# Attention on one Trainium2 core: weights times values in 512-query pieces, sums turned one head later, one norm spread over the steps

## The chip, the cores and the metric

One NeuronCore of one Trainium2 chip. The metric is the device time of one execution in microseconds. The kernel runs a chain of four layers on a sequence of 2 x 1024 tokens of width 256; the change touches only the last layer.

## The reference, cut to what it computes

```
x: 2 batches x 1024 tokens x 256
x = layer0(x); x = layer1(x); x = layer2(x)      # linear attention, two state-space layers
# layer 3, 16 heads of width 16
xn = layer_norm(x) * w + b
q, k, v = xn @ q_w + q_b, xn @ k_w + k_b, (xn @ v_w + v_b) * mask
att = softmax(q k^T + (1 - mask) * -1e6)          # per head, 1024 x 1024
y = att v                                         # per head, 1024 x 16
h = layer_norm(y) * g(cond) + h(cond)             # the norm called lny3 below
x + silu(h) @ out_w + out_b
```

## The kernel before, in words

Layer 3 handles 32 heads (2 batches x 16). Four heads make a unit (u = 0 to 7; units 0 to 3 are batch 0), and a unit has eight steps (mt = 0 to 7), one for each tile of 128 keys. So there are 64 steps, and in each the four heads j = 0 to 3 are taken in turn. All engines follow one written order; semaphores (`w.wait_ge`) join them.

For one head in one step TensorE computes the scores of 128 keys against 1024 queries: two bf16 matmuls of 512 columns (L1546) into a pair of PSUM banks. There are two such pairs (the ring `doubles`), so a pair is taken only when ScalarE has done the exponential of the head two places before (L1582, one ACTIVATE of 128x1024). The exponentials (the "weights") of one step lie in SBUF and are multiplied with the values in the step after it: `weigh_t` (L1408) does this as fp32 matmuls, the four heads side by side in four 32-column tiles of the array. Each fp32 matmul appears as two records. Before, `weigh_t(.., c)` handles 256 queries and one quarter c is issued at each head j, between the second trial and the second score matmul.

The exponential needs the maximum of each row, and that is computed ahead, LEAD = 40 items before it is used. An item is 128 queries of one head: two "trial" matmuls of 512 keys (L1360), each into one bank of a ring of only two (`first`), and two VectorE reductions (L1373, 128x512 from PSUM), each of which gives its bank back. One item goes with each head of each step, for the first 54 steps. Every eighth item also turns the collected maxima: an fp32 transpose (L1322) that takes a bank of the same ring, a copy on VectorE (L1328), and small work on GpSimd (L1336 to L1342) and two DMAs that bring the row into the operand of the scores.

The order on TensorE for one head is therefore: trial 0, score 0, trial 1, quarter c = j of the weights times values of the step before, score 1.

At the end of a unit the sums lie in two PSUM banks (PV). ScalarE copies one (`normalise_s`, L1425), VectorE the other (L1432), TensorE turns them with eight fp32 transposes into a pair of the ring `doubles` (`normalise_t`, L1418), and VectorE divides by the sum (L1437, L1440) and so frees the pair. Before, all of this stands after head 3 of the first step of the next unit.

When batch 0 is complete, its tail is put between the steps of units 5 and 6 (`tail_due`): lny3 of batch 0 after step (5, 1), its transposes and Silu after (5, 4), the four output products after (5, 7) to (6, 7). lny3 is `norm_v`: eight bn_stats (L205), eight bn_aggr (L208), one add (L210), a power on GpSimd (`norm_p`, L218), and eight tensor_scalar (L213) that subtract and scale; before, all but the power is VectorE's, in one piece. Batch 1 has its tail at the end.

Of the kernel before, what the change touches and what calls it, by code (L numbers as in the profile page):

```python
# [8 lines left out]
ALU = mybir.AluOpType  # L9
# [5 lines left out]
TB = S // 128  # L15
# [92 lines left out]
def program(nc, T, out):  # L108
    with ExitStack() as ctx:
# [18 lines left out]
        ST = sb("ST", [128, NT, 6])  # L128
        MV = sb("MV", [128, NT, 2])
# [67 lines left out]

        def norm_v(e, w, tag, src, dst, tiles, wait):  # L200
            a, b = tiles[0], tiles[-1] + 1
            w.wait_ge(*dve.now())
            for i in tiles:
                wait(i)
                e.bn_stats(ST[:, i, :], src(i)).then_inc(*dve.up((tag, "stats", i)))  # L205
            for i in tiles:
                w.wait_ge(*dve.at((tag, "stats", i)))
                e.bn_aggr(MV[:, i, :], ST[:, i, :]).then_inc(*dve.up())  # L208
            w.wait_ge(*dve.now())
            e.tensor_scalar(VE[:, a:b], MV[:, a:b, 1], EPS, None, ALU.add).then_inc(*dve.up((tag, "var")))  # L210
            w.wait_ge(*pool.at((tag, "rsqrt")))
            for i in tiles:
                e.tensor_scalar(dst(i), src(i), MV[:, i, 0:1], RS[:, i:i + 1], ALU.subtract, ALU.mult).then_inc(*dve.up((tag, i)))  # L213

        def norm_p(e, w, tag, tiles):
            a, b = tiles[0], tiles[-1] + 1
# [8 lines left out]
        def turn_t(e, w, tag, src, chunks, wait, ring=banks):  # L225
            for c in chunks:
                for h in range(2):
                    o = take(w, (tag, c, h), ring)
                    for j in range(4):
                        wait(4 * c + j)  # L230
                        t = e.transpose(o[:, j * 128:(j + 1) * 128], src(4 * c + j, h), ident[:, :])
                    t.then_inc(*pe.up((tag, c, h)))
# [1166 lines left out]
        def weigh_t(e, w, u, mt, c):  # L1399
            b, g = units[u]  # L1400
            for j in range(HQ):
                h, tile = HQ * g + j, b * TB + mt
                if mt == 0 and u:
                    w.wait_ge(*act.at(("lower", u - 1)))
                    w.wait_ge(*dve.at(("upper", u - 1)))
                w.wait_ge(*act.at(("weights", u, mt, j)))
                w.wait_ge(*act.at(("v3", tile)))
                t = e.matmul(PV[32 * j:32 * j + 32, c // 2, c % 2 * 256:c % 2 * 256 + 256], V[:, tile * 272 + 17 * h:tile * 272 + 17 * h + 32],  # L1408
                             PX[mt % 2][j][:, c * 256:(c + 1) * 256], start=mt == 0 and c % 2 == 0, stop=mt == TB - 1, tile_position=(0, 32 * j),
                             skip_group_check=True)  # L1410
            t.then_inc(*pe.up(("weighed", u, mt, c)))

# [6 lines left out]
            t.then_inc(*pe.up(("turned", u)))  # L1419

        def normalise_s(e, w, u):
            w.wait_ge(*pe.at(("weighed", u, TB - 1, 3)))
            if u:
                w.wait_ge(*pe.at(("turned", u - 1)))
            e.activation(PVs[:, 0:512], PV[:, 0, :], ACT.Copy).then_inc(*act.up(("lower", u)))  # L1425

        def normalise_v(e, w, u):
            b, g = units[u]
            w.wait_ge(*pe.at(("weighed", u, TB - 1, 3)))
            if u:  # L1430
                w.wait_ge(*pe.at(("turned", u - 1)))
            e.tensor_copy(PVs[:, 512:1024], PV[:, 1, :]).then_inc(*dve.up(("upper", u)))  # L1432
            i = banks.place.get(("turned", u), 2)
            f4 = PS[:, i:i + 2, :].rearrange("p a (q j e) -> p (a q) j e", j=HQ, e=32)
            w.wait_ge(*pe.at(("turned", u)))
            w.wait_ge(*dve.now())
            e.reciprocal(RC, f4[:, :, :, 16]).then_inc(*dve.up())  # L1437
            w.wait_ge(*dve.now())
            y = Yt[:, b * TB:(b + 1) * TB, HQ * 16 * g:HQ * 16 * (g + 1)].rearrange("p q (j e) -> p q j e", j=HQ)
            e.tensor_tensor(y, f4[:, :, :, 0:16], RC.unsqueeze(3).broadcast_to([128, TB, HQ, 16]), ALU.mult).then_inc(*dve.up(("y3", u)))  # L1440
            banks.give(("turned", u), dve.now())
# [2 lines left out]

        def tail_t(e, w, b, n, ring):
            if n == 1:
                turn_t(e, w, ("sn3", b), lambda i, h: Yt[:, i, h * 128:(h + 1) * 128], (2 * b, 2 * b + 1), lambda i: w.wait_ge(*dve.at((("lny3", b), i))), ring)
            if n >= 2:
                i = b * TB + 2 * (n - 2)
                w.wait_ge(*act.at((("sn3", b), i // 4, 1)))  # L1450
                tokens_t(e, w, ("o3", i), lambda k, i: SN[b][k][i // 4 % 2][:, i % 4 * 128:(i % 4 + 1) * 128], 2, lambda k: Wo[:, k, :], "l3bo",
                         (i, i + 1), ring)
# [44 lines left out]
        def layer3_p(e, w):  # L1497
            layer2_done(w)
            e.memset(V, 1.0).then_inc(*pool.up("v_ones"))
            norm3_p(e, w, 1)  # L1500
            for job in front_jobs(0):
                if not isinstance(job, int) and job[3] and job[4] and on_pool(*job[0:3]):
                    rest_of_parts(e, w, job, pool)
            todo = front_jobs(1)
            for i in range(LEAD):
                ahead_p(e, w, i)
                if i < len(todo) and not isinstance(todo[i], int) and todo[i][3] and todo[i][4]:
                    rest_of_parts(e, w, todo[i], pool)
            for u, mt, last in steps():
                for j in range(HQ):  # L1510
                    ahead_p(e, w, LEAD + 32 * u + 4 * mt + j)
                if tail_due(u, mt) is not None:
                    tail_p(e, w, 0, tail_due(u, mt))
            for n in range(6):
                tail_p(e, w, 1, n)

        def layer3_t(e, w):
# [17 lines left out]
            for u, mt, last in steps():  # L1535
                for j in range(HQ):
                    k = HQ * u + j
                    sl = k % SLOTS
                    key = ("score", u, mt, j)
                    take(w, key, doubles)  # L1540
                    for c in range(2):
                        ahead_t(e, w, LEAD + 32 * u + 4 * mt + j, (c,))
                        if c == 1 and last:
                            weigh_t(e, w, *last, j)
                        w.wait_ge(*transfer(f"max_row{sl}").at(k))
                        t = e.matmul(PS[:, banks.place[key] + c, :], SK3[sl][0:102, mt * 128:(mt + 1) * 128], SQ[sl][0:102, c * 512:(c + 1) * 512],  # L1546
                                     start=True, stop=True)
                    t.then_inc(*pe.up(key))
                    if last and j == 3 and last[1] == TB - 1:
                        normalise_t(e, w, last[0])  # L1550
                if tail_due(u, mt) is not None:
                    tail_t(e, w, 0, tail_due(u, mt), doubles)
            for c in range(4):
                weigh_t(e, w, len(units) - 1, TB - 1, c)
            normalise_t(e, w, len(units) - 1)
            w.wait_ge(*dve.at(("y3", len(units) - 1)))
# [4 lines left out]
        def layer3_s(e, w):  # L1561
# [12 lines left out]
            for u, mt, last in steps():  # L1574
                for j in range(HQ):
                    key = ("score", u, mt, j)
                    i = banks.place.get(key, 2)
                    w.wait_ge(*pe.at(key))
                    step = 8 * u + mt
                    if step >= 2:  # L1580
                        w.wait_ge(*pe.at(("weighed", (step - 2) // 8, (step - 2) % 8, 3)))
                    e.activation(PX[mt % 2][j], PS[:, i:i + 2, :].rearrange("p a b -> p (a b)"), ACT.Exp).then_inc(*act.up(("weights", u, mt, j)))  # L1582
                    banks.give(key, act.now())
                    if last and j == 3 and last[1] == TB - 1:
                        normalise_s(e, w, last[0])
                if tail_due(u, mt) is not None:
                    tail_s(e, w, 0, tail_due(u, mt))
            normalise_s(e, w, len(units) - 1)
# [3 lines left out]
        def layer3_v(e, w):  # L1592
# [14 lines left out]
            for u, mt, last in steps():  # L1607
                for j in range(HQ):
                    for c in range(2):
                        ahead_v(e, w, LEAD + 32 * u + 4 * mt + j, (c,))  # L1610
                    if last and j == 3 and last[1] == TB - 1:
                        normalise_v(e, w, last[0])
                if tail_due(u, mt) is not None:
                    tail_v(e, w, 0, tail_due(u, mt))
            normalise_v(e, w, len(units) - 1)
            for n in range(6):
                tail_v(e, w, 1, n)
# [132 lines left out]
```

## Time and profile before

| | |
|---|---|
| time, median of 3 runs | 2215.05 us (2214.99 to 2222.23) |
| profiled execution, its own time | 2217.42 us |
| its span, first to last instruction | 2215.7 us |
| mean granted TensorE clock | 0.949 |
| attention steps, first to last exponential | 1715.1 to 2183.1 us |
| one step, from first exponential to first exponential | 6.69 or 6.91 us (with a turn of maxima) |
| DVE, ACT, POOL busy over 1713 to 2186 us (473 us) | 309.25, 271.11, 40.81 us |

A row of the timeline gives the start, the length, the engine, the line, the operation and its operands, and how often it was merged; in brackets stands how long the engine was idle before it and what released it. PE is TensorE's matmul, PEld its weight load, DVE VectorE, ACT ScalarE, POOL GpSimd; x8 means eight records merged into one row. The records of matmuls are longer than the spacing of their starts, because matmuls are pipelined; so the starts are what is to be compared. PEclk is the granted clock of TensorE: 1.00 is 2.4 GHz, 0.50 is 1.2 GHz.

### The profile page before, as it was taken

How to read it: one execution, taken by the hardware profiler on the slowest of the kernel's cores; microseconds unless marked ns; L12 is line 12 of the kernel's file. 1: busy time of each engine (PE TensorE's matmuls, PEld its weight loads, DVE VectorE, ACT ScalarE, POOL GpSimd, SP SyncE). 2: the span in 40 equal slices, each digit the busy share in tenths (PEclk: the TensorE clock that was granted, in tenths of full speed). 3: DMA queues.
4: the chain of work that ended last, by engine and by line, in shares of the span. 5: the costliest groups of instructions: out<-in, count | busy, mean ns of one | idle time of the engine just before them, and what ended most of it. 6: DMA issues, size and time to landing. Idle time of an engine off the chain costs nothing.

```text
span 2215.7 us, 34737 instructions
## 1 busy us (share of the span) xinstructions
PE 2018.9 (91%) x13528; PEld 1417.9 (64%) x13528; DVE 1613.1 (73%) x2067; ACT 1438.8 (65%) x2422; POOL 1061.2 (48%) x594
## 2 busy tenths in 40 slices
PE   6969799887998899989999999899988999998997
PEld 4844699737997499759984899599842222332333
DVE  5554699447996499769984899599768777776621
ACT  3314799347983699589845997799642655554564
POOL 1021499405994199639950799299624100111000
PEclk9989799987999899999999999999998999998998
DMA  4040111101111011102100111111101111111000
GB/s 175 1 141 20 43 58 58 41 13 55 58 57 50 20 54 58 35 23 55 54 24 2 49 58 49 35 54 58 29 22 38 30 29 30 29 28 30 9 20 20
DMA packets 54161, 95.04 MB, mean 43 GB/s; under 512 B 11815, under 2 KB 20167, under 8 KB 52590
## 3 DMA queue, kind: packets, MB, share of 16 engines
q1 hardware_dynamic: 52462, 88.63, 13.2%
q0 software_dynamic: 1536, 4.20, 0.6%
q8 instruction: 107, 1.75, 0.3%
q14 instruction: 56, 0.46, 0.1%
HBM read 73.29 MB, written 6.91 MB: 36 GB/s over the span
## 4 chain that ended last, share of the span: by engine, by line
PE 66%; POOL 8%; ACT 8%; DVE 8%; issue 8%; DMA 1%; SPq 0%; POOLq 0%; DVEq 0%; ACTq 0%
PE PS L723 11%; PE PS L745 11%; POOL A L857 7%; PE PS L1408 6%; PE PS L253 5%; PE PS L1360 5%; PE PS L1546 5%; PE PS L728 5%; PE PS L244 4%; PE PS L608 2%; PE PS L751 2%; ACT A L809 2%; PE PS L1090 1%; DVE A L1029 1%; DVE A L1373 1%
## 5 line engine op out<-in xcount | busy, mean ns | idle before, releaser
L857 POOL TENSOR_TENSOR A<-A 128x1024 f32<-128x1024 f32 x384 | 897.9, 2391 | 138.1 <-ACT small L798 126.1
L809 ACT ACTIVATE A<-A,negA 128x512 f32<-128x512 f32 x768 | 546.6, 712 | 42.5 <-DVE A L842 32.9
L842 DVE TENSOR_TENSOR_SCAN A<-A,PS 128x512 f32<-128x512 f32 x384 | 434.4, 1199 | 55.0 <-ACT A L809 36.3
L842 DVE TENSOR_TENSOR_SCAN A<-A,small,PS 128x512 f32<-128x512 f32 x384 | 455.2, 1256 | 6.1 <-PE PS L723 5.5
L745 PE MATMUL PS<-ident,A 128*128 128x128 f32 x3072 | 401.3, 273 | 18.8 <-POOL A L857 13.8
L1582 ACT ACTIVATE A<-PS 128x1024 f32<-128x1024 f32 x256 | 262.2, 1024 | 222.0 <-PE PS L1546 220.4
L723 PE MATMUL PS<-A 128*128 128x128 f32 x3072 | 392.4, 280 | 5.6 <-DVE A L842 5.6
L1373 DVE TENSOR_REDUCE A<-PS 128x1 f32<-128x512 f32 x512 | 329.8, 686 | 80.7 <-PE PS L1360 77.3
L723 PEld LDWEIGHTS PS<-A 128*128 128x128 f32 x3072 | 371.5, 196 | 14.2 <-DVE A L842 7.8
L745 PEld LDWEIGHTS PS<-ident,A 128*128 128x128 f32 x3072 | 346.6, 141 | 28.8 <-POOL A L857 19.0
L783 ACT ACTIVATE A<-A,small 128x512 f32<-128x512 f32 x340 | 239.9, 710 | 24.3 <-PE PS L728 20.2
L728 PE MATMUL PS<-ident,A 128*128 128x128 f32 x1360 | 195.5, 282 | 24.7 <-ACT A L783 23.8
L1360 PE MATMUL PS<-A 99*128 99x512 bf16 x480 | 189.4, 401 | 8.0 <-DVE A L1373 7.2
L1408 PE MATMUL PS<-A,W 128*32 128x256 f32 x2048 | 192.5, 397 | 1.7 <-ACT A L1582 1.7
L1546 PE MATMUL PS<-A 102*128 102x512 bf16 x480 | 184.9, 392 | 0.1
L728 PEld LDWEIGHTS PS<-ident,A 128*128 128x128 f32 x1360 | 163.0, 146 | 32.9 <-issue 22.8
L790 ACT ACTIVATE A<-ident,small 128x128 f32<-128x128 f32 x384 | 147.4, 388 | 7.5 <-PE PS L723 6.7
L218 POOL TENSOR_TENSOR RS<-VE,HALF 128x8 f32<-128x8 f32 x14 | 23.0, 1644 | 265.6 <-DVE VE L210 265.6
L685 POOL TENSOR_TENSOR A<-A 128x2048 f32<-128x2048 f32 x6 | 32.2, 5374 | 241.8 <-ACT A L647 241.8
L244 PE MATMUL PS<-A,W 128*128 128x512 f32 (+1 forms) x288 | 132.0, 616 | 8.9 <-ACT A L1014 6.6
L1546 PEld LDWEIGHTS PS<-A 102*128 102x128 bf16 x480 | 46.4, 98 | 126.2 <-issue 100.6
L1408 PEld LDWEIGHTS PS<-A,W 128*32 128x32 f32 x2048 | 47.8, 109 | 121.6 <-issue 99.3
(198 smaller groups left out, 2045.5 us busy)
## 6 DMA issues: line engine op xcount, KB each, us to landing
A<-scrc SPq DMA_DIRECT2D x192, 256.0 KB, 3.1
A<-A SPq DMA_DIRECT2D x360, 32.0 KB
scr<-A SPq DMA_DIRECT2D x4, 1024.0 KB, 4.6
W<-in_wa SPq DMA_DIRECT2D x2, 1536.0 KB, 10.1
X<-in_x SPq DMA_DIRECT2D x4, 512.0 KB, 5.4
out<-X SPq DMA_DIRECT2D x2, 1024.0 KB, 4.5
W<-in_w SPq DMA_DIRECT2D x1, 1984.0 KB, 8.3
W<-in_wzc SPq DMA_DIRECT2D x1, 1536.0 KB, 11.8
```

What stands on the lines that cost most here:

```text
L723: t = e.matmul(o[:, j * 128:(j + 1) * 128], r.DUT[:, 4 * ci + j, dt * 128:(dt + 1) * 128], DB[k // 2 % 2][:, j, :], start=True, stop=True)
L728: t = e.transpose(o[:, j * 128:(j + 1) * 128], r.G[(2 * k + j) % 6][:, dt * 128:(dt + 1) * 128], ident[:, :])
L745: t = e.matmul(PS[:, j, dt * 128:(dt + 1) * 128], r.H[pair % HS][:, dt % 2, j * 128:(j + 1) * 128], ident[:, :], start=open_y(ci, j), stop ...
L783: e.activation(r.G[(2 * k + j) % 6], r.DUT[:, 4 * ci + j, :], ACT.Copy, scale=Bt[:, 4 * ci + j, s:s + 1]).then_inc(*scaled.up((q, k, j)))
L809: e.activation(A_B[i % 4], r.DT[:, dt, ci * 512:(ci + 1) * 512], ACT.Exp, scale=negA[:, r.n, dt * 16 + s:dt * 16 + s + 1]).then_inc(*decay ...
L842: e.tensor_tensor_scan(h, a, u, init, ALU.mult, ALU.add).then_inc(*scanned.up((q, i)))
L857: e.tensor_tensor(h, h, CB[k % 2].unsqueeze(1).broadcast_to([128, 2, 512]), ALU.mult).then_inc(*weighed.up((q, pair)))
L1360: e.matmul(o, SQ[j][0:99, nt * 128:(nt + 1) * 128], SK3[j][0:99, c * 512:(c + 1) * 512], start=True, stop=True).then_inc(*pe.up(("trial", ...
L1373: e.tensor_reduce(NM[:, k % 2, q:q + 1], bank(("trial", k, nt, c)), AX.X, ALU.max, negate=True).then_inc(*dve.up(("trial", k, nt, c)))
L1408: t = e.matmul(PV[32 * j:32 * j + 32, c // 2, c % 2 * 256:c % 2 * 256 + 256], V[:, tile * 272 + 17 * h:tile * 272 + 17 * h + 32], PX[mt % ...
L1546: t = e.matmul(PS[:, banks.place[key] + c, :], SK3[sl][0:102, mt * 128:(mt + 1) * 128], SQ[sl][0:102, c * 512:(c + 1) * 512], start=True, ...
L1582: e.activation(PX[mt % 2][j], PS[:, i:i + 2, :].rearrange("p a b -> p (a b)"), ACT.Exp).then_inc(*act.up(("weights", u, mt, j)))
```

## The change

1. `weigh_t` handles 512 queries instead of 256: `c` runs over 2 instead of 4, one PSUM bank each. It is issued at j = 1 (c = 0) and j = 3 (c = 1) only.
2. The end of a unit is spread. The copy by ScalarE comes before the exponential of head 3 of step (u, 0), the copy by VectorE after the reductions of that head, and the transposes and the division one head later, at j = 0 of step (u, 1).
3. lny3 of batch 0: two bn_stats after each of the steps (4, 3) to (4, 6), the aggregation after (4, 7), the power and the eight tensor_scalar on GpSimd, there too. Batch 1's norm keeps its order.

```diff
+        def stats_v(e, tag, src, tiles):
+            for i in tiles:
+                e.bn_stats(ST[:, i, :], src(i)).then_inc(*dve.up((tag, "stats", i)))
...
+        def moments_v(e, w, tag, tiles):       # the bn_aggr and the add of norm_v, moved here
...
-                t = e.matmul(PV[32 * j:32 * j + 32, c // 2, c % 2 * 256:c % 2 * 256 + 256], V[:, tile * 272 + 17 * h:tile * 272 + 17 * h + 32],
-                             PX[mt % 2][j][:, c * 256:(c + 1) * 256], start=mt == 0 and c % 2 == 0, stop=mt == TB - 1, tile_position=(0, 32 * j),
+                t = e.matmul(PV[32 * j:32 * j + 32, c, :], V[:, tile * 272 + 17 * h:tile * 272 + 17 * h + 32],
+                             PX[mt % 2][j][:, c * 512:(c + 1) * 512], start=mt == 0, stop=mt == TB - 1, tile_position=(0, 32 * j),
...
         def normalise_v(e, w, u):              # the copy is now take_upper_v
-            w.wait_ge(*dve.now())
+            if u:
+                w.wait_ge(*dve.at(("y3", u - 1)))
...
 # layer3_p
-                if tail_due(u, mt) is not None:
-                    tail_p(e, w, 0, tail_due(u, mt))
+                if u == 4 and mt == 7:
+                    tail_p(e, w, 0, 0)
+                    w.wait_ge(*pool.at((("lny3", 0), "rsqrt")))
+                    for i in range(TB):
+                        e.tensor_scalar(Yt[:, i, :], Yt[:, i, :], MV[:, i, 0:1], RS[:, i:i + 1], ALU.subtract, ALU.mult).then_inc(*pool.up(("lny3", 0, i)))
...
 # layer3_t
-                        if c == 1 and last:
-                            weigh_t(e, w, *last, j)
+                        if c == 1 and last and j % 2:
+                            weigh_t(e, w, *last, j // 2)
...
-                    if last and j == 3 and last[1] == TB - 1:
-                        normalise_t(e, w, last[0])
+                    if j == 0 and u and mt == 1:
+                        normalise_t(e, w, u - 1)
...
 # layer3_s
+                    if j == 3 and u and mt == 0:
+                        normalise_s(e, w, u - 1)
                     w.wait_ge(*pe.at(key))
...
-                    if last and j == 3 and last[1] == TB - 1:
-                        normalise_s(e, w, last[0])
...
 # layer3_v
-                    if last and j == 3 and last[1] == TB - 1:
-                        normalise_v(e, w, last[0])
-                if tail_due(u, mt) is not None:
+                    if j == 3 and u and mt == 0:
+                        take_upper_v(e, w, u - 1)
+                    if j == 0 and u and mt == 1:
+                        normalise_v(e, w, u - 1)
+                if u == 4 and 3 <= mt < 7:
+                    w.wait_ge(*dve.at(("y3", 3)))
+                    stats_v(e, ("lny3", 0), lambda i: Yt[:, i, :], (2 * mt - 6, 2 * mt - 5))
+                if u == 4 and mt == 7:
+                    moments_v(e, w, ("lny3", 0), range(TB))
+                if tail_due(u, mt):
                     tail_v(e, w, 0, tail_due(u, mt))
```

## Rows read from the trace of the kernel before

**Rows 1.** Two heads of a regular step, TensorE, VectorE and ScalarE (timeline).

```profile
1803.45 0.38 PE L1360 MATMUL PS<-A 99*128 99x512 bf16 x1
1803.76 0.64 PE L1408 MATMUL PS<-A,W 128*32 128x256 f32 x8
1804.33 0.39 PE L1546 MATMUL PS<-A 102*128 102x512 bf16 x1
1804.56 0.38 PE L1360 MATMUL PS<-A 99*128 99x512 bf16 x1
1804.76 1.02 ACT L1582 ACTIVATE A<-PS 128x1024 f32<-128x1024 f32 x1 [0.52 <-PE PS L1546]
1804.97 1.29 DVE L1373 TENSOR_REDUCE A<-PS 128x1 f32<-128x512 f32 x2 [0.26 <-PE PS L1360]
...
1805.83 0.14 PEld L1408 LDWEIGHTS PS<-A,W 128*32 128x32 f32 x2 [0.38 <-ACT A L1582]
```

**Rows 2.** First exponential of two steps that lie two apart, ScalarE (timeline).

```profile
1799.90 1.02 ACT L1582 ACTIVATE A<-PS 128x1024 f32<-128x1024 f32 x1 [1.03 <-PE PS L1546]
...
1813.50 1.02 ACT L1582 ACTIVATE A<-PS 128x1024 f32<-128x1024 f32 x1 [1.03 <-PE PS L1546]
```

**Rows 3.** A whole fp32 matmul of 512 columns and its successor, TensorE (timeline).

```profile
1660.00 1.02 PE L1248 MATMUL PS<-A,W 128*128 128x512 f32 x2
1660.87 0.73 PE L1360 MATMUL PS<-A 99*128 99x512 bf16 x2
```

**Rows 4.** A bank given back by VectorE and the weight load behind it (timeline).

```profile
1786.41 0.28 DVE L1328 COPY W<-PS 8x128 f32<-8x128 f32 x1 [0.66 <-PE PS L1322]
...
1786.74 0.10 PEld L1360 LDWEIGHTS PS<-W 99*128 99x128 bf16 x1 [0.43 <-DVE W L1328]
```

**Rows 5.** End of unit 0, all three engines (timeline).

```profile
1769.88 1.02 ACT L1582 ACTIVATE A<-PS 128x1024 f32<-128x1024 f32 x1 [1.03 <-PE PS L1546]
...
1774.32 0.39 PE L1546 MATMUL PS<-A 102*128 102x512 bf16 x1
...
1775.66 0.59 ACT L1425 ACTIVATE W<-PS 128x512 f32<-128x512 f32 x1
...
1776.40 1.06 PE L1418 MATMUL PS<-ident,W 128*128 128x128 f32 x8 [1.69 <-ACT W L1425]
...
1779.04 1.02 ACT L1582 ACTIVATE A<-PS 128x1024 f32<-128x1024 f32 x1 [2.79 <-PE PS L1546]
...
1786.30 1.02 ACT L1582 ACTIVATE A<-PS 128x1024 f32<-128x1024 f32 x1 [1.03 <-PE PS L1546]
```

**Rows 6.** First exponential after the end of unit 3, ScalarE (timeline).

```profile
1952.29 1.02 ACT L1582 ACTIVATE A<-PS 128x1024 f32<-128x1024 f32 x1 [4.36 <-PE PS L1546]
```

**Rows 7.** Around lny3 of batch 0 (timeline).

```profile
2015.40 2.71 DVE L205 BATCH_NORM_STATS2 ST<-A 128x6 f32<-128x256 f32 x8
...
2017.26 1.02 ACT L1582 ACTIVATE A<-PS 128x1024 f32<-128x1024 f32 x1 [1.03 <-PE PS L1546]
...
2020.61 2.67 DVE L213 TENSOR_SCALAR A<-A,MV,RS 128x256 f32<-128x256 f32 x8 [1.75 <-POOL RS L218]
...
2030.41 1.02 ACT L1582 ACTIVATE A<-PS 128x1024 f32<-128x1024 f32 x1 [1.81 <-PE PS L1546]
...
2034.10 1.02 ACT L1582 ACTIVATE A<-PS 128x1024 f32<-128x1024 f32 x1 [1.03 <-PE PS L1546]
```

**Rows 8.** Two stretches (windows): us; PE, PEld, DVE, ACT, POOL busy; PEclk; DMA; GB/s.

```profile
1706.00:1712.00 6.00, 5.26 (x9) 0.83 (x9) 5.59 (x9) 0.00 (x0) 0.00 (x0) 0.50 0.17 39
...
2024.00:2030.00 6.00, 5.77 (x25) 1.26 (x26) 3.43 (x6) 1.02 (x1) 1.40 (x4) 0.50 0.12 28
```

**Rows 9.** First exponentials of two steps without trials, ScalarE (timeline).

```profile
2151.81 2.13 ACT L1582 ACTIVATE A<-PS 128x1024 f32<-128x1024 f32 x2 [1.03 <-PE PS L1546]
...
2157.36 2.13 ACT L1582 ACTIVATE A<-PS 128x1024 f32<-128x1024 f32 x2 [1.03 <-PE PS L1546]
```

**Rows 10.** GpSimd's elementwise work in the layers before (page, costliest groups).

```profile
L857 POOL TENSOR_TENSOR A<-A 128x1024 f32<-128x1024 f32 x384 | 897.9, 2391 | 138.1 <-ACT small L798 126.1
```

More of the change, by code:

```diff
@@ L204, in norm_v @@
                 wait(i)
-                e.bn_stats(ST[:, i, :], src(i)).then_inc(*dve.up((tag, "stats", i)))
+                stats_v(e, tag, src, (i,))
+            moments_v(e, w, tag, tiles)
+            w.wait_ge(*pool.at((tag, "rsqrt")))
+            for i in tiles:
+                e.tensor_scalar(dst(i), src(i), MV[:, i, 0:1], RS[:, i:i + 1], ALU.subtract, ALU.mult).then_inc(*dve.up((tag, i)))
+        def moments_v(e, w, tag, tiles):
+            a, b = tiles[0], tiles[-1] + 1
             for i in tiles:
@@ L210, in norm_v @@
             e.tensor_scalar(VE[:, a:b], MV[:, a:b, 1], EPS, None, ALU.add).then_inc(*dve.up((tag, "var")))
-            w.wait_ge(*pool.at((tag, "rsqrt")))
-            for i in tiles:
-                e.tensor_scalar(dst(i), src(i), MV[:, i, 0:1], RS[:, i:i + 1], ALU.subtract, ALU.mult).then_inc(*dve.up((tag, i)))
         def norm_p(e, w, tag, tiles):
@@ L1421, in normalise_s @@
         def normalise_s(e, w, u):
-            w.wait_ge(*pe.at(("weighed", u, TB - 1, 3)))
+            w.wait_ge(*pe.at(("weighed", u, TB - 1, 1)))
             if u:
@@ L1425, in normalise_s, with take_upper_v @@
             e.activation(PVs[:, 0:512], PV[:, 0, :], ACT.Copy).then_inc(*act.up(("lower", u)))
-        def normalise_v(e, w, u):
-            b, g = units[u]
-            w.wait_ge(*pe.at(("weighed", u, TB - 1, 3)))
+        def take_upper_v(e, w, u):
+            w.wait_ge(*pe.at(("weighed", u, TB - 1, 1)))
             if u:
@@ L1432, in normalise_v @@
             e.tensor_copy(PVs[:, 512:1024], PV[:, 1, :]).then_inc(*dve.up(("upper", u)))
+        def normalise_v(e, w, u):
+            b, g = units[u]
             i = banks.place.get(("turned", u), 2)
@@ L1446, in tail_t @@
             if n == 1:
-                turn_t(e, w, ("sn3", b), lambda i, h: Yt[:, i, h * 128:(h + 1) * 128], (2 * b, 2 * b + 1), lambda i: w.wait_ge(*dve.at((("lny3", b), i))), ring)
+                turn_t(e, w, ("sn3", b), lambda i, h: Yt[:, i, h * 128:(h + 1) * 128], (2 * b, 2 * b + 1), lambda i: w.wait_ge(*(dve if b else pool).at((("lny3", b), i) if b else ("lny3", 0, i))), ring)
             if n >= 2:
@@ L1548, in layer3_t @@
                     t.then_inc(*pe.up(key))
-                    if last and j == 3 and last[1] == TB - 1:
-                        normalise_t(e, w, last[0])
+                    if j == 0 and u and mt == 1:
+                        normalise_t(e, w, u - 1)
                 if tail_due(u, mt) is not None:
                     tail_t(e, w, 0, tail_due(u, mt), doubles)
-            for c in range(4):
+            for c in range(2):
                 weigh_t(e, w, len(units) - 1, TB - 1, c)
@@ L1580, in layer3_s @@
                     if step >= 2:
-                        w.wait_ge(*pe.at(("weighed", (step - 2) // 8, (step - 2) % 8, 3)))
+                        w.wait_ge(*pe.at(("weighed", (step - 2) // 8, (step - 2) % 8, 1)))
                     e.activation(PX[mt % 2][j], PS[:, i:i + 2, :].rearrange("p a b -> p (a b)"), ACT.Exp).then_inc(*act.up(("weights", u, mt, j)))
                     banks.give(key, act.now())
-                    if last and j == 3 and last[1] == TB - 1:
-                        normalise_s(e, w, last[0])
                 if tail_due(u, mt) is not None:
@@ L1610, in layer3_v @@
                         ahead_v(e, w, LEAD + 32 * u + 4 * mt + j, (c,))
-                    if last and j == 3 and last[1] == TB - 1:
-                        normalise_v(e, w, last[0])
-                if tail_due(u, mt) is not None:
+                    if j == 3 and u and mt == 0:
[8 more added lines that the diff above has]
+                if tail_due(u, mt):
                     tail_v(e, w, 0, tail_due(u, mt))
+            take_upper_v(e, w, len(units) - 1)
             normalise_v(e, w, len(units) - 1)
```

## The prediction

> **What bounds the kernel now.** I read the page for where the time lies, then the timeline of the attention steps engine by engine, then windows for the granted clock. The reader is to look at starts, not lengths. In a regular step TensorE is the bound: from the trial at 1803.45 to the scores at 1804.33 and the next trial at 1804.56 nothing but issue stands between matmuls, and a head repeats after 1.54 us (the exponential takes 1.02 after 0.52 us of idling for its scores) [rows 1]. Of that, four bf16 matmuls take 0.22 each and the quarter of the weights times values 0.66 (1803.45 to 1804.33, less 0.22). Once in a step it also waits: the first quarter needs the exponential of head 3, started just before: its last weight load comes at 1805.83, when that exponential (1804.76 + 1.02) ends [rows 1], and the next exponential then idles 1.03 instead of 0.52 [rows 2]. That makes 3 x 1.545 + 2.05 = 6.69 us a step; two steps take 13.60 [rows 2], so one with a turn of maxima takes 6.91. VectorE's two reductions take 1.29 of the 1.54 us [rows 1]: close behind.
>
> **The weights times values alone.** A quarter is four fp32 matmuls side by side. A whole fp32 matmul of 512 columns passes in 0.87 us [rows 3], so 256 columns stream in 0.43, and 0.66 - 0.43 = 0.23 us is fixed: 0.09 on entry (0.31 from the trial to it, less 0.22), the rest inside and on leaving. A half of 512 columns should cost 0.86 + 0.23 = 1.09, of which 1.00 from its own start to the scores behind it. Two halves are 2.18 us a step against 2.64: 0.46 less. Also the half now stands at head 1, when the exponential of head 3 is long done: 0.51 less. On TensorE's account a step falls from 6.69 to 5.72. No row shows four side by side at 512 columns. From below it can't be under its streaming, 0.86; from above, a half costs two quarters from start to scores, 2 x 0.57 = 1.14 [rows 1]. I take 1.00, since streaming scaled in rows 3.
>
> **What the step really does then.** The trials have two banks. Count from trial 0 of an even head, which has no half: its reductions start 0.42 later and take 1.29 [rows 1], and a bank given back lets the next weight load start 0.05 later [rows 4]. So trial 1 of the odd head, which needs the second of these banks, starts at 0.42 + 1.29 + 0.05 = 1.76, although TensorE would be there at 1.3. Then the half: 0.31 to its start, 1.00 to score 1, 0.22 to the next trial. A pair of heads takes 3.30 and a step 6.59, against 6.69. In a step with a turn of maxima the turn takes one of the two banks, so the gate moves from trial 1 to trial 0, 0.44 earlier in the order: 6.59 + 0.44 = 7.03, against 6.91. The steps alternate, so the two cancel (-0.10 and +0.12, some 20 pairs: **+0.5**). Nearly the whole 0.97 us per step is given to this gate: before, a quarter lay at every head and covered it; now even heads have no cover and odd heads have twice too much. The first step loses a wait and gains **-0.8**.
>
> **End of a unit.** Before: two steps take 16.42 us (1769.88 to 1786.30) where 13.60 is regular [rows 2, 5], 2.8 more. TensorE idles from 1774.54 (0.22 after the scores) to 1776.40, for the exponential of head 3 and ScalarE's copy behind it, then works 0.90 on the transposes, and the trial behind waits for the division on VectorE. After: ScalarE copies (0.59 [rows 5]) between the end of the half and the exponential of head 3, which so starts 0.45 after score 1 (0.43 before [rows 1]) and ends at 1.47. TensorE goes on with head 0 of the next step and is through at 0.22 + 4 x 0.22 = 1.10; the transposes then take the pair of banks that this exponential gives back, so they wait some 0.4 and take 0.9. The gate of the next odd head, 0.3 or so, would have been waited for anyway. That is 1.0 more than regular, so -1.8 for each of six ends, and -0.7 at the last, where no trials lie: **-11.5**; I take **-11**.
>
> **The norm.** Before, lny3 holds VectorE for 7.9 us in one piece, 2015.40 to 2023.28, with the two reductions waiting behind it and TensorE behind them; the step takes 16.84 (2017.26 to 2034.10) [rows 7]. Afterwards it is a regular 7.03: **-9.8**, of which 2.6 is half clock after the stall: PEclk is 0.50 from 2024 to 2030 [rows 8], and a head takes 1.81 + 1.02 = 2.83 us there [rows 7] instead of 1.54, twice. What comes instead: two bn_stats in each of four steps, 0.68 us (2.71 for eight [rows 7]) behind the last reduction, on the gate's chain only in part: **+0.4**. The subtraction on GpSimd: from below as VectorE, 2.7 us for eight [rows 7]; from above as its two-input work, 2.39 us per 1024 elements [rows 10], 4.8 for eight, with its start some 6. Its results are first needed after step (5, 4), 30 us later, and the row maxima queued behind it on GpSimd are for a head used 40 items later. Cost nothing; if a step did wait, at most these 6 us.
>
> **Tail of batch 0 and the steps without trials.** Six pieces lie between steps; after each the first head has no half, so the gate is not covered: 0.4 each, **+2.3**. After Silu the exponential's table returns while TensorE now has no quarter to do: **+0.8**. From the last trial on, a pair of heads must wait for the exponential two places before: 1.02 + 0.05 + 1.31 + 0.43 = 2.81, a step 5.62 against 5.56 [rows 1, 9]; and the last step's halves both lie behind its last exponential's partner: **+1.8** together.
>
> **Clock at the ends of units.** At the end of unit 3 the exponentials idle for 4.36 us [rows 6] where they idle for 2.79 at the end of unit 0 [rows 5]. The work is the same; the 1.6 us are half clock, and the end of unit 4 has them too. With 0.4 us idle instead of 1.9 I expect both gone: **-3.2** (bound: 0).
>
> **Sum.** +0.5 - 0.8 - 11 - 9.8 + 0.4 + 2.3 + 0.8 + 1.8 - 3.2 = **-19.0 us**. The profiled execution (2217.4, span 2215.7) would be 2198.4; it lies 2.4 above the median, which becomes 2196. 0.5% (11 us) is what a measurement of this kernel can tell from no change.
>
> **A rule that speaks against it.** With the gate, TensorE waits on PSUM banks twice in each pair of heads. While trials ran alone, gated in just that way, PEclk was 0.50 [rows 8]. The Trainium skill (TensorE: Matmul & The Clock Gate, "A second HAM failure mode: psum-queue depth-cycling") says that such short idles between groups can make the clock fall and rise again. By that rule the steps would pay the half clock often, as in rival 3. I give it little, because the new step streams 16 x 0.22 + 2 x 0.86 = 5.2 of its 6.6 us [rows 1, 3]; the old one streamed the same in 6.7, without losing the clock.
>
> **Rivals.**
> 1. The half is dear, or a release takes longer than 0.05. With 1.14 for 1.00 each of some 125 halves costs 0.14 on the chain: +18, so 2214. Halfway: 2205. For it: nobody ran this form. Against: rows 3. Chance 0.20, ends within 0.5%.
> 2. The whole gain on TensorE arrives, since the gate is less tight than I count: 0.97 x 54 steps = 52 instead of nothing, 2145. Against it stand VectorE's 1.29 us and two banks. Chance 0.04.
> 3. **The other side:** the clock falls to 1.2 GHz in the steps because of the gate's idles. At half clock a head takes 2.83 us instead of 1.54 [rows 1, 7], 1.3 more. From 15 of the 256 heads on the gain of 19 is gone, from 23 on the kernel is slower by over 0.5%; with one head in six halved it is 43 x 1.3 = +56 on 2196, 2252. Chance 0.06.
> 4. The norm's new places hurt: GpSimd's 6 us are waited for, and the statistics fall wholly on the chain (4 x 0.7): +9, 2205. Chance 0.08, within or just faster.
>
> **How the numbers follow.** The forecast, 2196, has 0.62. Its own terms leave -12 to -26. Range 2184 to 2213: below, the half at its streaming (-0.1 x 125 = -12); above, rival 1 nearly whole. Faster by over 0.5%: the forecast, rival 2, and some of 1 and 4: 0.72; same: 0.21; slower: 0.07.
>
> **What would show it.** Half to scores 1.00 us; regular steps 6.6 and 7.0, with idle time before the odd heads' trial 1 put down to the reduction; ends of units 14.6 for two steps; step (5, 1) near 7.0; no PEclk under 1 at the ends of units 3 and 4. The forecast is wrong if steps are near 5.8 (the gate isn't one) or over 6.8 (half or release dearer), or if PEclk falls in regular steps.

## The result, and the profile after

The changed kernel takes 2203.06 us (median of 6 runs, 2194.13 to 2205.47), the kernel before on the same chip 2216.49 (6 runs, 2213.74 to 2223.2): a ratio of 0.9924, 95% interval 0.9899 to 0.9949. It is faster by 0.76%. The prediction said 2196 with a range of 2184 to 2213: right in direction and range, 7 us too low. In a later series of runs, against the kernel before of that series, it stands at 0.9900 (0.9867 to 0.9933).

Two questions follow. Did the gain come from where the prediction put it? And why did the time fall by 13.4 us and not by 19?

**Where the time went.** The two kernels share all code up to the attention stage. I take the stretch from the first exponential to the last from ScalarE's timeline; it holds all that the change touches but the end of the last unit. Before it runs from 1715.06 to 2183.11, 468.0 us. After:

```profile
1723.11 1.02 ACT L1598 ACTIVATE A<-PS 128x1024 f32<-128x1024 f32 x1 [24.16 <-PE PS L1560]
...
2171.86 1.02 ACT L1598 ACTIVATE A<-PS 128x1024 f32<-128x1024 f32 x1 [0.89 <-PE PS L1560]
```

That is 448.8 us, 19.3 less by the unrounded records; the forecast sum was 19.0. But the first exponential comes 8.05 us later than before, in code that nobody changed. Windows of both kernels over layer 2 show the clearest part of it (us; PE, PEld, DVE, ACT, POOL busy; PEclk; DMA; GB/s), after and then before:

```profile
1390.00:1412.00 22.00, 21.48 (x37) 8.33 (x38) 7.09 (x9) 14.34 (x16) 0.00 (x0) 0.61 0.02 4
```

```profile
1389.00:1411.00 22.00, 21.36 (x55) 8.31 (x55) 11.90 (x10) 18.25 (x21) 4.32 (x1) 1.00 0.02 4
```

The reader is to see the same place in the program at PEclk 0.61 against 1.00. The chain that ended last has the same 16 matmuls there (one line of the program, eight lines lower in the changed file), after and before:

```profile
1390.52 11.55 PE PS L616 x16
...
1422.62 1.93 PE PS L1098 x4
```

```profile
1389.64 7.13 PE PS L608 x16
...
1413.52 1.93 PE PS L1090 x4
```

From the first row to the last the changed kernel falls from 0.88 us behind to 9.10 us behind. So the profiled execution after (2205.47, span 2203.7) is 12.0 us under the one before (2217.42, span 2215.7), and not 19: 19.3 less the 8.05, and 0.7 us that it is shorter behind the last exponential (31.9 for 32.6).

**The regular step.** TensorE, VectorE and ScalarE in two heads of the changed kernel (timeline), which answer to [rows 1] and [rows 2]:

```profile
1821.77 0.38 PE L1368 MATMUL PS<-A 99*128 99x512 bf16 x1
1821.99 0.38 PE L1560 MATMUL PS<-A 102*128 102x512 bf16 x1
1822.21 0.38 PE L1368 MATMUL PS<-A 99*128 99x512 bf16 x1
1822.43 0.38 PE L1560 MATMUL PS<-A 102*128 102x512 bf16 x1
1823.05 0.39 PE L1368 MATMUL PS<-A 99*128 99x512 bf16 x1 [0.24 <-ACT A L1598]
1823.28 0.38 PE L1560 MATMUL PS<-A 102*128 102x512 bf16 x1
1823.53 0.39 PE L1368 MATMUL PS<-A 99*128 99x512 bf16 x1
1823.85 1.06 PE L1416 MATMUL PS<-A,W 128*32 128x512 f32 x8
1824.85 0.39 PE L1560 MATMUL PS<-A 102*128 102x512 bf16 x1
```

```profile
1821.97 1.94 ACT L1598 ACTIVATE A<-PS 128x1024 f32<-128x1024 f32 x2 [1.81 <-PE PS L1560]
1822.19 2.58 DVE L1381 TENSOR_REDUCE A<-PS 128x1 f32<-128x512 f32 x4 [0.68 <-PE PS L1368]
1823.53 0.10 PEld L1368 LDWEIGHTS PS<-A 99*128 99x128 bf16 x1 [0.37 <-DVE A L1381]
1825.28 1.94 ACT L1598 ACTIVATE A<-PS 128x1024 f32<-128x1024 f32 x2 [1.37 <-PE PS L1560]
```

The half goes from its start to the scores in 1.00 us (1823.85 to 1824.85), as forecast from a whole matmul [rows 3]. Then two rings are to be read. A ring is here a set of banks that are used in turn, and its length is the time from the taking of a bank to the moment at which the same bank can be taken again. Both come to 3.3 us for a pair of heads.

- The trials' banks: trial 0 of the even head at 1821.77, its reductions from 1822.19 (0.42), two of them 1.29, the next weight load at 1823.53 (0.05): 1.76 us, to the hundredth what was forecast. Then 0.32, 1.00 and 0.22 to the next even head: 3.30.
- The scores' banks: the exponential of the odd head starts at 1821.97 and takes 1.02; 0.06 later, at 1823.05, the next odd head's trial 0 starts, for in program order the head takes its pair of score banks ahead of its trials. Then 0.23 + 0.25 + 0.32 + 1.00 to the last scores and 0.43 to their exponential at 1825.28: 3.31, of which 0.03 is the wait of trial 1 for the first ring.

The prediction saw the first and not the second, and in these heads the idle time stands at the second's place. The waits over 1723 to 2172 (us in total, times, longest) say so for the whole stage, in which the waits for the reduction are the fewer:

```profile
PE PS L1368 <- ACT A L1598: 15.8, 65, 0.2
PE PS L1368 <- DVE A L1381: 6.3, 27, 0.6
```

**The steps.** Durations from first exponential to first exponential. A regular step takes 6.62 and one with a turn of maxima 7.05, against 6.69 and 6.91. Sorted by the prediction's terms, with the differences of all 64 steps (steps beside a piece of the tail count as tail, those at the end of a unit as ends):

| term | forecast | measured |
|---|---|---|
| regular steps | +0.5 | +0.9 (34 steps) |
| first step | -0.8 | -1.0 |
| ends of units with their half clock | -11 - 3.2 | -13.2 (-1.6 for each of units 0 to 2, -2.6, -2.7, -1.1, -1.9) |
| norm's step | -9.8 | -9.8 (16.85 to 7.06) |
| statistics | +0.4 | +0.2 |
| tail pieces, table | +2.3 + 0.8 | +1.8 |
| steps without trials, last step | +1.8 | +1.8 (0.09 for each of six, 1.2) |
| sum | -19.0 | -19.3 |

An end of a unit on TensorE and ScalarE (timeline), which answers to [rows 5]:

```profile
1838.52 0.39 PE L1560 MATMUL PS<-A 102*128 102x512 bf16 x1
1838.66 0.60 ACT L1433 ACTIVATE W<-PS 128x512 f32<-128x512 f32 x1 [1.08 <-PE PS L1416]
1839.15 1.94 ACT L1598 ACTIVATE A<-PS 128x1024 f32<-128x1024 f32 x2
1840.22 1.09 PE L1426 MATMUL PS<-ident,W 128*128 128x128 f32 x8 [0.44 <-ACT A L1598]
1841.15 0.38 PE L1368 MATMUL PS<-A 99*128 99x512 bf16 x1
```

TensorE idles 0.44 us in front of the transposes, where it idled 1.69 in [rows 5] (the row's own mark), and the trial follows at once. The exponential after the end of unit 3 idles 2.24 us where it idled 4.36 [rows 6], the same as after unit 1:

```profile
1843.33 2.03 ACT L1598 ACTIVATE A<-PS 128x1024 f32<-128x1024 f32 x2 [2.24 <-PE PS L1560]
...
1954.94 2.03 ACT L1598 ACTIVATE A<-PS 128x1024 f32<-128x1024 f32 x2 [2.24 <-PE PS L1560]
```

The half clock is gone from the ends. The stage begins at half clock in both kernels (until 1727.6 here and 1719.8 before, by the clock's records). After that it falls in one place only. The windows show the whole stage and the stretch with that place (columns as above):

```profile
1723.00:2172.00 449.00, 400.28 (x2091) 110.04 (x2093) 303.43 (x528) 257.62 (x269) 50.23 (x121) 0.99 0.11 25
...
2034.00:2048.00 14.00, 11.52 (x61) 4.56 (x53) 6.13 (x11) 10.06 (x11) 0.00 (x0) 0.88 0.00 0
```

The second holds the tail's transposes and Silu, not regular steps.

### The profile page after: what moved, and what is told of

Same layout as the page of the kernel before. It is cut to its first block, busy times and chain, and to the rows that moved or that the text cites. A ratio compares the mean times of both kernels' runs of the same rounds, so it can differ in the third digit from the quotient of the medians.

```text
span 2203.7 us, 32728 instructions
## 1 busy us (share of the span) xinstructions
PE 1984.2 (90%) x12504; PEld 1392.5 (63%) x12504; DVE 1609.2 (73%) x2059; ACT 1426.4 (65%) x2422; POOL 1068.6 (48%) x602
## 3 DMA queue, kind: packets, MB, share of 16 engines
q1 hardware_dynamic: 52462, 88.63, 13.4%
HBM read 73.29 MB, written 6.91 MB: 36 GB/s over the span
## 4 chain that ended last, share of the span: by engine, by line
PE 63%; ACT 11%; DVE 9%; POOL 8%; issue 7%; DMA 1%; SPq 0%; POOLq 0%; DVEq 0%; ACTq 0%
PE PS L731 11%; PE PS L753 11%; POOL A L865 7%; PE PS L261 5%; PE PS L736 5%; PE PS L1416 5%; PE PS L1368 4%; PE PS L252 4%; ACT A L1598 4%; PE PS L1560 3%; DVE A L1381 3%; PE PS L616 2%; PE PS L759 2%; ACT A L817 2%; PE PS L1098 2%
## 5 line engine op out<-in xcount | busy, mean ns | idle before, releaser
L1598 ACT ACTIVATE A<-PS 128x1024 f32<-128x1024 f32 x256 | 249.5, 1021 | 207.7 <-PE PS L1560 207.7
L1560 PE MATMUL PS<-A 102*128 102x512 bf16 x480 | 179.4, 387 | 12.5 <-ACT A L1598 12.2
L1416 PE MATMUL PS<-A,W 128*32 128x512 f32 x1024 | 137.2, 605 | 0.1
L1368 PEld LDWEIGHTS PS<-A 99*128 99x128 bf16 x480 | 46.8, 98 | 142.6 <-DVE A L1381 74.9
```

The lines of the kernel that those rows point to most:

```text
L1368: e.matmul(o, SQ[j][0:99, nt * 128:(nt + 1) * 128], SK3[j][0:99, c * 512:(c + 1) * 512], start=True, stop=True).then_inc(*pe.up(("trial", ...
L1416: t = e.matmul(PV[32 * j:32 * j + 32, c, :], V[:, tile * 272 + 17 * h:tile * 272 + 17 * h + 32], PX[mt % 2][j][:, c * 512:(c + 1) * 512], ...
```

## The experiments

Each is read by the stretch between first and last exponential and by its steps, since the layers in front of it end at another time in each run (below). Three series, each on one chip with runs of the kernel before: quarters kept, halves alone, norm spread alone and the changed kernel again (before: 2220.57); half reductions, both halved and the two with moved pieces (2217.49); half exponentials and ends spread alone (2218.32).

**1. The pieces of the weights times values alone, one way and the other.** First the changed kernel with the quarters of the kernel before, one at each head (the excerpts of code are shortened at the marks).

```diff
-                t = e.matmul(PV[32 * j:32 * j + 32, c, :], V[...],
-                             PX[mt % 2][j][:, c * 512:(c + 1) * 512], start=mt == 0, ...
+                t = e.matmul(PV[32 * j:32 * j + 32, c // 2, c % 2 * 256:c % 2 * 256 + 256], V[...],
+                             PX[mt % 2][j][:, c * 256:(c + 1) * 256], start=mt == 0 and c % 2 == 0, ...
...
-                        if c == 1 and last and j % 2:
-                            weigh_t(e, w, *last, j // 2)
+                        if c == 1 and last:
+                            weigh_t(e, w, *last, j)
```

> The changed kernel, but with the weights times values in 256-query quarters at every head, as before; the end of a unit and the norm stay spread. Theory A (two banks for the trials and two pairs for the scores set the pace of the steps, so the halves bring nothing): regular steps 6.69 and 6.91 us, end of a unit 15.0 us for its two steps, step (5, 1) 6.9, the stretch from first to last exponential about 1.5 us SHORTER than in the changed kernel's profile (448.8), so some 447, and the time equal to the changed kernel's or 1 to 2 us less. Theory B (the halves bring a real part of the gain, their saved fixed costs of 0.46 us a step): the stretch 10 us or more longer than 448.8.

Measured: 2192.53 us (2184.58 to 2193.15), ratio 0.9873 (0.9833 to 0.9912); the unaltered changed kernel beside it 2194.71. The stretch is 447.7 us against 448.5 in the changed kernel's run of that series. Steps 6.69 and 6.91, ends of units 15.24, the norm's step 6.91, steps without trials 5.56. The other way round, the kernel before with the halves alone:

> The kernel before, with the halves alone: 512 queries at heads 1 and 3; unit ends and norm as before. Theory A: regular steps 6.6 and 7.05, which cancel; ends of units dearer by 0.7 us each, since a wait on the last half is longer; the stretch from first to last exponential some 10 us LONGER than before's 468.0, about 478, and the kernel slower than before by about 0.4%. Theory B: the stretch 10 to 30 us shorter than 468.

Measured: 2227.3 us (2211.2 to 2230.46), ratio 1.0018 (0.9986 to 1.0051); stretch 476.4, 8.3 more than before. Steps 6.62 and 7.05 as in the changed kernel, but an end of a unit is 17.20 against 16.41 (+4.7 for all seven), and tail, steps without trials and last step cost +2.0, +0.5 and +1.2. What follows: the halves bring nothing on balance. Inside the changed kernel they cost about 1 us, alone 8 us, and the difference lies at the ends of units: they make the old end dearer by 4.7 us in all and the spread one cheaper by 2.3 (14.79 each for 15.24 with quarters). The gain is that of the other two parts.

**2. The other two parts alone**, both with quarters. The norm spread, the ends as before (the excerpt is against the changed kernel; ScalarE's and VectorE's parts go back to the same place, and the quarters are as in experiment 1):

```diff
-                    if j == 0 and u and mt == 1:
-                        normalise_t(e, w, u - 1)
+                    if last and j == 3 and last[1] == TB - 1:
+                        normalise_t(e, w, last[0])
...
```

> The kernel before, with only lny3 of batch 0 spread over the steps and scaled on GpSimd. Both theories: step (5, 1) 6.9 us instead of 16.85, steps (4, 4) and (4, 6) and (5, 0) up by 0.1 to 0.4 us, the stretch from first to last exponential 468.0 - 9.3 = 458.7. A rival, that the work on GpSimd is waited for, would show as a wait of a transpose of lny3 on GpSimd after step (5, 4).

Measured: 2204.39 us (one run), stretch 459.25: -8.8. The norm's step is 6.91, ends 9.16 and 7.25 as before, and after units 1 to 3 10.7 to 10.8 and 6.69 with half clock in them. The norm's step alone gave -9.9; the ends, where half clock now falls at other units, took 2.2 back. And the ends spread, the norm in one piece as before (part 2 of the change, on the kernel before):

> The kernel before with only the unit ends spread; quarters of 256 queries, the norm in one piece. Regular steps 6.69 and 6.91 us; the two steps at a unit's end 15.05 to 15.2 us instead of 16.4, or 17.4 where the old end lost the clock; step (5, 1) still 16 to 17 us. The stretch from first to last exponential 468.0 - 8.3 by the chain of waits, and up to 4.4 less where the half clock at the ends of units 3, 4 and 6 goes with them: 455 to 460. If the spread only moved the wait to the next step, it would stay at 466 or more.

Measured: 2209.69 us (one run), stretch 455.6: -12.4. Ends 7.11 and 8.13, the norm's step 15.74. The seven ends give -10.8 of it and the norm's step -1.1. The two kernels sum to -21.2, together (quarters kept) they give -20.4. So they add up within 0.8. The norm is near its terms of the forecast (-9.8 + 0.4); the ends stay 1.8 short of theirs (-11 - 3.2), which counted on the halves.

**3. The changed kernel again**, for how far the unchanged layers move.

> The changed kernel as it is, once more. The attention steps should take 448.8 us again within 0.2. What is open is the 8 us by which its layers 0 to 2, which the change leaves alone, came later in the profile: if that is where half-clock stretches happen to fall, this run's own offset of the first exponential (1723.1 then, 1715.1 before) may be either, near 1715 or near 1723, and single times fall in two groups some 8 us apart, near 2195 and near 2203. If it belongs to the changed program, it is near 1723 again and no time is near 2195.

Measured: 2194.71 us (2187.24 to 2202.14), ratio 0.9900. The profiled execution has the same stretch as the first, 448.5 against 448.8, but its first exponential comes at 1704.9 and not at 1723.1. The single times don't fall in two groups as expected; they spread from 2187 to 2202. The views of the cores show span and clock of the two:

```profile
core 0: 2203.7 us, clock 0.947
```

```profile
core 0: 2185.5 us, clock 0.961
```

The time at half clock ahead of the first exponential, added up from the clock's records, is 214.0 us in the first and 152.3 in the second. Ten of the twelve profiles execute the same instructions up to there (the two kernels with half reductions, below, don't: the reductions of the first 40 items lie ahead of the first exponential). In these ten it comes between 1704.6 us (152.3 at half clock) and 1723.2 (214.0), and the order by time is the order by time at half clock without an exception. The kernel before had 1715.1 and 186.4.

**4. Which ring sets the pace.** The reductions over 256 instead of 512 columns; this leaves half of each row out of the maxima.

```diff
-                e.tensor_reduce(NM[:, k % 2, q:q + 1], bank(("trial", k, nt, c)), AX.X...
+                e.tensor_reduce(NM[:, k % 2, q:q + 1], bank(("trial", k, nt, c))[:, 0:256], AX.X...
```

> The changed kernel with each of VectorE's reductions over 256 of its 512 keys only, so the maximum subtracted is one of half the row (part of the computation is left out). Theory A (two rings of about equal tightness: the two banks of the trials, and the two pairs of the scores, which wait for the exponential two heads before): with the first ring eased, the second holds a pair of heads at 1.02 + 0.06 + the four matmuls and the half to score 1 with its 0.43: regular steps fall only to 6.5 and 6.7 us, a little over half of what the bank of the trials costs in the steps with a turn and almost nothing in the others. Theory C (the trials' banks are the only gate): steps of 5.7 to 5.8 and 6.0 us.

Measured: 2163.49 us (one run), stretch 434.65. Steps 6.52 and 6.73: 0.10 and 0.32 less. Next the exponentials of 512 queries only; the weights of the other half are not computed.

```diff
-                    e.activation(PX[mt % 2][j], PS[:, i:i + 2, :].rearrange("p a b -> p (a b)"), ACT.Exp)...
+                    e.activation(PX[mt % 2][j][:, 0:512], PS[:, i, :], ACT.Exp)...
```

> The changed kernel with each exponential over 512 of its 1024 queries only (the other weights stay what they were), the reductions whole. Theory A, with the trials' banks as the tighter ring in the regular steps: nothing changes there, 6.62 and 7.05 us, while steps without trials fall from 5.65 to 4.8 and the second step of a unit from 7.55 to 7.2. If the exponential's ring were the tighter one: 6.5 and 6.8 or less.

Measured: 2192.55 us (one run), stretch 436.55. Regular steps stay at 6.62 and 7.05. Steps without trials fall from 5.65 to 4.79, and an end of a unit from 14.79 to 14.36; these and the tail of batch 0 make up the 12.2 us of the stretch. Then both edits in one:

> The same, and each exponential over 512 of its 1024 queries only (the rest of the weights stays what it was), so ScalarE's instruction is about 0.6 us. Both rings are eased. Theory A: TensorE's own account remains, 16 x 0.22 + 2 x 1.09 = 5.7 us for a regular step and some 6.15 or less with a turn of maxima; the stretch from first to last exponential about 392 us instead of 448.6. Steps that stay above 6.3 would say that a half costs more than 1.09, or that something else holds them. Steps without trials: 4.8 us instead of 5.65.

Measured: 2137.57 us (one run), stretch 398.3, where 392 was expected. Steps 5.91 and 6.27. Its TensorE (timeline) names nothing that it waits for:

```profile
1800.97 0.38 PE L1560 MATMUL PS<-A 102*128 102x512 bf16 x1
1801.30 0.38 PE L1368 MATMUL PS<-A 99*128 99x512 bf16 x1
1801.52 0.38 PE L1560 MATMUL PS<-A 102*128 102x512 bf16 x1
1801.73 0.38 PE L1368 MATMUL PS<-A 99*128 99x512 bf16 x1
1802.04 1.07 PE L1416 MATMUL PS<-A,W 128*32 128x512 f32 x8
1803.04 0.39 PE L1560 MATMUL PS<-A 102*128 102x512 bf16 x1
```

What follows: taking one ring's work away frees at most 0.1 us in a step without a turn of maxima, taking both away 0.71. There two rings tie. In a step with a turn the trials' banks are the tighter ring: half reductions free 0.32 and half exponentials nothing. The arithmetic of the second ring holds as well: without the wait of trial 1 it is 1.02 + 0.06 + 0.22 + 0.22 + 0.31 + 1.00 + 0.43 = 3.26 a pair, 6.52 a step, which is the step with half reductions. TensorE's own account, forecast at 5.72, measured 5.91; twice a step a matmul starts 0.11 later than the usual 0.22 after its forerunner (1800.97 to 1801.30), at the odd head's trial 0.

**5. Other places for the same work.** If both rings run through the half, then a half ahead of the point where the head takes its banks should be outside the scores' ring and lie under its wait.

```diff
+                    if last and j in (1, 2):
+                        weigh_t(e, w, *last, (1, 2).index(j))
                     take(w, key, doubles)
                     for c in range(2):
                         ahead_t(e, w, LEAD + 32 * u + 4 * mt + j, (c,))
-                        if c == 1 and last and j % 2:
-                            weigh_t(e, w, *last, j // 2)
```

> The changed kernel with the two halves at other places: before the pair of banks is taken and trial 0 of head 1, and the same at head 2. Nothing else changes. By theory A the halves then lie where TensorE would otherwise wait for VectorE and ScalarE: regular steps 6.55 and 6.76 us instead of 6.62 and 7.05, steps without trials 5.3 instead of 5.65, the stretch from first to last exponential 448.6 - 11.7 = 437, and the time 0.5% under the changed kernel's. If the size of the half alone mattered and not its place, nothing changes.

Measured: 2176.57 us (2166.62 to 2181.74), ratio 0.9805 (0.9779 to 0.9832); stretch 432.2, 16.6 less than the changed kernel. Steps 6.53 and 6.74, ends 14.30, steps without trials 5.15. The stretch was expected at 437; the regular steps came as expected (6.55 and 6.76) and give 6.0 of the 16.6 us, the ends 4.4, the steps without trials 3.3, tail and last step 2.8. ScalarE's timeline shows the four gaps of a regular step with a turn, uneven now:

```profile
1839.26 1.02 ACT L1598 ACTIVATE A<-PS 128x1024 f32<-128x1024 f32 x1 [1.16 <-PE PS L1560]
1841.23 1.02 ACT L1598 ACTIVATE A<-PS 128x1024 f32<-128x1024 f32 x1 [0.95 <-PE PS L1560]
1842.57 1.02 ACT L1598 ACTIVATE A<-PS 128x1024 f32<-128x1024 f32 x1 [0.31 <-PE PS L1560]
1843.82 1.02 ACT L1598 ACTIVATE A<-PS 128x1024 f32<-128x1024 f32 x1 [0.23 <-PE PS L1560]
```

and TensorE's what still stops it in that step, the reduction, where no half lies between two heads:

```profile
1841.41 0.38 PE L1368 MATMUL PS<-A 99*128 99x512 bf16 x1 [0.22 <-DVE A L1381]
```

Last, quarters in the changed kernel with only the first of them moved, from head 0, where it waits for head 3's exponential, to the front of head 1:

```diff
+                    if last and j == 1:
+                        weigh_t(e, w, *last, 0)
                     take(w, key, doubles)
...
-                        if c == 1 and last:
+                        if c == 1 and last and j:
                             weigh_t(e, w, *last, j)
```

> Quarters of 256 queries at every head with the spread unit ends and norm, and only quarter 0 moved: from between trial 1 and score 1 of head 0 to before trial 0 of head 1, when the exponential of head 3 is done. Theory A: its 0.5 us of waiting in each step is replaced by less: regular steps 6.56 and 6.78 us instead of 6.69 and 6.91, steps without trials 5.4, the stretch 447.7 - 9.3 = 438.4, level with the halves at their better places. So the size of the pieces brings nothing of its own here. If the halves' saved fixed costs counted, this one would be 10 us or more behind them.

Measured: 2179.15 us (2170.23 to 2185.3), ratio 0.9838 (0.9820 to 0.9855); stretch 431.9, where 438.4 was expected. Steps 6.47 and 6.68 against 6.69 and 6.91 with all quarters in their old places, ends 14.39 against 15.24. The place of the pieces is worth some 16 us with either size (447.7 to 431.9 with quarters, 448.8 to 432.2 with halves), and at these places the size is worth nothing. Both kernels beat the one before, and by their ratios (intervals up to 0.9832 and 0.9855) the changed one too (0.9867 and up in its two series). The rows above show which wait is left with the halves; what paces the steps at the new places no run takes apart, and why the two gained 5 and 6.5 us more than expected stays open.

## Why the prediction came out as it did

**The decomposition was right.** The terms sum to -19.0 and the stage lost 19.3, with no term more than 1.3 us off. The norm's -9.8 and the ends' -11 - 3.2 (measured -13.2) were the whole gain, as the prediction said; experiment 2 shows each by itself. Two sizes inside the ends were off and cancelled in part. The half clock at the ends of units 3 and 4 was worth 2.1 us and not 3.2: the two steps there took 17.42 and 17.46 us before where the ends of units 0 to 2 took 16.41, for the step behind the stall is 0.56 shorter (6.69 for 7.25), and the prediction read only the stall. And the last end gained 1.9 where 0.7 was forecast.

**The halves' nothing was right, its mechanism half right.** The prediction gave nearly all of the 0.97 us a step on TensorE to the trials' banks and reckoned 3.30 us a pair. The rows show that ring at exactly that length, and in the steps with a turn it is the one that paces (forecast 7.03, measured 7.05). But its sign in the profile, "idle time before the odd heads' trial 1 put down to the reduction", did not come: trial 1 starts 0.03 late, and the 0.24 us of idling is at trial 0, put down to the exponential. The step that failed is the count of rings: the prediction considered the scores' banks for the steps without trials alone (5.62, measured 5.65) and not for the regular ones, where the same ring is 3.26 to 3.31 long. The number survived by luck, because the two tie; the advice that one would have drawn from it ("make the reductions cheaper") is worth 0.1 us a step without a turn, as the half reductions showed.

**The size of the time was missed outside the change.** 19 us were forecast, 12.0 seen between the two profiled executions and 13.4 between the medians. The interval of the ratio reaches from -11.3 to -22.4 us, so the medians don't contradict 19. Between the profiled executions the missing 7 us are shown: 8 us lie ahead of the first exponential, in unchanged code, with 214.0 us at half clock in one and 186.4 in the other, and 0.7 came back at the end. What decides there whether the clock falls is open; no run tried it. The prediction took the layers ahead as fixed, and its range held the error.

**Rivals.** 1, a dear half or release: refuted, 1.00 us and 0.05 us. 2, the whole gain on TensorE: refuted for this kernel; experiment 4 shows that it needs both rings gone, and then a step is 5.91. 3, the clock falls in the steps: refuted, PEclk is 0.99 over the stage, and what is lost lies at its first 4.5 us and at the tail's transposes. The rule on depth-cycling that the prediction weighed (the Trainium skill, TensorE: Matmul & The Clock Gate, "A second HAM failure mode: psum-queue depth-cycling") says that short idles of TensorE between groups of matmuls, as it goes round its PSUM banks, can make the clock fall. This trace has such idles, 65 for the exponential and 27 for the reduction in front of trials, and no fall in the regular steps. 4, the norm's new places: not paid, though GpSimd was far slower than bounded. Its timeline:

```profile
1999.91 1.64 POOL L226 TENSOR_TENSOR RS<-VE,HALF 128x8 f32<-128x8 f32 x1 [10.82 <-DVE VE L221]
2001.65 9.65 POOL L1527 TENSOR_SCALAR A<-A,MV,RS 128x256 f32<-128x256 f32 x8
2011.27 0.28 POOL L1344 CAST A<-W 8x128 bf16<-8x128 f32 x1
```

11.3 us in all where some 6 were forecast. Its users, the transposes, come at 2034.84, over 23 us later. The maxima that queued behind it until 2011.27 were not waited for either: no row of the waits over 1723 to 2172 names GpSimd as what was waited for. The norm's old step, from 2015.23 on (by the count of exponentials (5, 2); the prediction called it (5, 1)), is 7.06. The cover, and not the price, made this term right.

## What to carry to other kernels

When one engine's work is made cheaper, write down every ring of buffers through which it passes, from take to give back and to take again, and not only the engine that is next busiest: here two rings of 3.30 and 3.26 us held a pair of heads that took TensorE 2.95 once both were eased. If rings tie, shortening one shows next to nothing; moving a piece of TensorE's work ahead of the point where the next buffers are taken gave 16 us for no work saved. Judge a change of one stage by that stage's own stretch, since stages that nobody touched can move by more than the gain.

## What the runs showed of the hardware that was not expected

GpSimd's subtraction and multiplication with two values per partition took 1.21 us for 128 x 256 fp32 (9.65 for eight). My upper bound, 0.6 from the two-input rows [rows 10], was too low by a factor of two, and VectorE does one in 0.33 [rows 7]. The same instructions ahead of the first exponential ended anywhere between 1704.6 and 1723.2 us over ten executions of nine kernels, with 152 to 214 us of it at the half clock. And where neither bank ring stops TensorE, an odd head's first trial still starts 0.33 us after its forerunner instead of 0.22, twice a step (1800.97 to 1801.30 above); what it waits for there no row names.
